# First attention phase: GpSimd subtracts the row maximum before the transposes, ScalarE applies the exponential behind them, and builds the masked queries

## The reference, cut to what matters

```python
scores = einsum('bhqd,bhkd->bhqk', qh, kh) + mask          # layer 0
scores = where(mask == 0, -inf, clip(scores * scale, -100, 100))   # layer 1
weights = softmax(scores, axis=-1)
ctx = einsum('bhqk,bhkd->bhqd', weights, vh)
```

## Time and profile before

| | us |
|---|---|
| runs of the kernel before | 2157.89, 2166.70, 2175.78 |
| their median | 2166.70 |
| span of the profiled execution, first to last instruction | 2161.6 |
| median less span | 5.1 |
| first phase in that execution | about 46 to 875 |

### The profile page before, as it was taken

How to read it: one execution, slowest core, us unless ns; L and a number is a source line. 1 busy time by engine, 2 the same in 40 slices (tenths; PEclk the granted TensorE clock), 3 DMA queues, 4 the chain that set the end, 5 groups by cost and what they waited for, 6 DMA issues and landing times.

```text
span 2161.6 us, 49950 instructions
## 1 busy us (share of the span) xinstructions
PE 1864.7 (86%) x17665; PEld 1517.8 (70%) x17669; DVE 1485.2 (69%) x3873; ACT 1300.1 (60%) x4466; POOL 616.4 (29%) x610
## 2 busy tenths in 40 slices
PE   3987988888889999648788989999999998898878
PEld 2776877777778777536666667777787777676765
DVE  5887776786877888566776676776767565564456
ACT  1886655565556688436677766666666654554432
POOL 0003021241312230014343434244353533333221
PEclk9998999999999999867799999999999999999999
DMA  8013334463444310210000011232222223232351
GB/s 240 17 31 102 106 114 144 130 180 96 141 128 140 102 31 7 96 64 20 24 25 2 20 39 33 83 92 66 89 62 80 82 70 105 61 96 79 99 155 51
DMA packets 119637, 178.44 MB, mean 83 GB/s; under 512 B 9824, under 2 KB 77728, under 8 KB 119136
## 3 DMA queue, kind: packets, MB, share of 16 engines
q1 hardware_dynamic: 111712, 159.51, 24.6%
q0 software_dynamic: 7680, 15.74, 2.5%
HBM read 141.26 MB, written 33.95 MB: 81 GB/s over the span
## 4 chain that ended last, share of the span: by engine, by line
PE 37%; DVE 9%; ACT 5%; issue 4%; POOL 1%; DMA 0%; DVEq 0%; ACTq 0%; SPq 0%
PE ps L1659 5%; PE ps L1944 5%; PE ps L1892 3%; PE ps L1697 3%; PE ps L1885 3%; ACT pb L2093 2%; PE ps L1681 2%; PE ps L1866 2%; PE ps L1688 2%; PE ps L1670 2%; PE ps L1707 1%; DVE nm L2472 1%; PE ps L1715 1%; PE ps L1914 1%; PE ps L1858 1%
## 5 line engine op out<-in xcount | busy, mean ns | idle before, releaser
L2093 ACT ACTIVATE pb<-ps,nm 128x128 f32<-128x128 f32 x1024 | 363.2, 377 | 194.1 <-DVE nm L2472 194.0
L2141 POOL TENSOR_TENSOR pb<-pb,rcs 128x512 f32<-128x512 f32 x256 | 267.8, 1047 | 661.6 <-DVE rcs L2480 660.8
L981 ACT ACTIVATE pb<-pb,nm 128x128 f32<-128x128 f32 x1024 | 313.0, 393 | 52.1 <-DVE nm L1206 50.6
L2497 DVE COPY pt<-ps 128x512 f32<-128x512 f32 x128 | 88.2, 689 | 198.0 <-PE ps L1944 197.9
L2093 ACT ACTIVATION_READ_ACCUMULATOR pb<-ps,nm 128x1 f32 x1024 | 221.8, 217 | 0.0
L2472 DVE TENSOR_REDUCE nm<-ps 128x8 f32<-128x1024 f32 x128 | 155.8, 1217 | 61.9 <-PE ps L1892 38.7
L1944 PE MATMUL ps<-w,pb 128*128 128x128 f32 x1024 | 168.3, 290 | 21.4 <-ACT pt L2101 10.2
L1206 DVE TENSOR_REDUCE nm<-pb 128x8 f32<-128x1024 f32 x128 | 156.1, 1220 | 4.4
L1944 PEld LDWEIGHTS ps<-w,pb 128*128 128x128 f32 x1024 | 122.2, 148 | 45.1 <-ACT pt L2101 19.3
L865 PE MATMUL ps<-w,pb 128*128 128x128 f32 x1024 | 146.0, 286 | 6.8 <-ACT pb L981 6.6
L2101 ACT ACTIVATE pt<-ps 128x512 f32<-128x512 f32 x128 | 76.9, 601 | 92.9 <-PE ps L1944 92.8
(11 more groups left out here) (379 smaller groups left out, 4415.6 us busy)
## 6 DMA issues: line engine op xcount, KB each, us to landing
big<-in_we SPq DMA_DIRECT2D x92, 514.0 KB, 3.7
big<-in_we SPq DMA_DIRECT2D x109, 384.0 KB, 3.1
sorted_out<-big SPq DMA_DIRECT2D x27, 256.0 KB
big<-sorted_in SPq DMA_DIRECT2D x7, 960.0 KB, 5.8
sorted_in<-big SPq DMA_DIRECT2D x4, 1472.0 KB, 12.2
hidden<-h_all SPq DMA_DIRECT2D x7, 512.0 KB, 3.0
h_all<-hidden SPq DMA_DIRECT2D x7, 512.0 KB, 3.8
sorted_out<-h_all SPq DMA_DIRECT2D x14, 256.0 KB
```

What stands on the lines that cost most here:

```text
L981: m = a.activation(pb[:, n % 2, k * S:(k + 1) * S], pb[:, n % 2, k * S:(k + 1) * S], ACT.Exp, bias=nm[:, n % 2, k:k + 1])
L2093: m = a.activation(pb[:, n % 2, e * S:(e + 1) * S], ps[:, score_bank(n) + half, k * S:(k + 1) * S], ACT.Exp, bias=nm[:, n % 2, e:e + 1], a ...
L2141: g_.tensor_tensor(p4, p4, r4.unsqueeze(2).to_broadcast([P, 4, S]), ALU.mult).then_inc(n2["p_normed"], 1)
L2497: v.tensor_copy(pt[:, p % 2, 4 * S:8 * S], ps[:, BANK_T, :]).then_inc(n2["p_lo"], 1)
```

## The change

- GpSimd adds nm to pb, in place, for each half of a unit (new function `shift`, semaphore `shifted`), at the head of its loop's turn n.
- PE's transposes wait for `shifted` in place of `exps`; so does DVE's maximum, which reuses nm.
- ACT's eight exponentials of a unit are gone. It empties both banks of the transposed values with Exp, in all units; DVE's copy is gone.
- `queries` moves from DVE to ACT, to place 2 of u = 4 (layer 0) or u = 6 (layer 1).
- The gathers, so far all at u = 0, stand at u = 0, 1 and 2 (2, 3 and 3 of them). The scatters, so far four in each of u = 4 to 7, are three in each of six units from unit 27 (then 43, 59, 75) on; the sixth has one.

```diff
+        GATHERS = {0: range(0, 2), 1: range(2, 5), 2: range(5, 8)}
+        SCATTERS = [range(3 * i, min(3 * i + 3, 2 * PB)) for i in range(6)]
+        SCATTERS_FROM = 3 * NU + 3
@@ PE @@
-                                pe.wait_ge(s["exps"], 2 * p + 1 + k // 4)
+                                pe.wait_ge(s["shifted"], 2 * p + 1 + k // 4)
@@ ACT @@
+                    if layer == 0 and here == (2, 4):
+                        queries(j + 1, (front.yT_ready, g + 1), W("hm"))
+                    if layer == 1 and here == (2, 6):
+                        queries(j + 1, (s["q_col"], g + 1), W("hms"))
+                def queries(j, there, heads_mask):
+                    a.wait_ge(*there)
+                    if j >= 2:
+                        a.wait_ge(s["scores"], NU * (j - 1))
+                    for i in range(4):
+                        m = a.activation(qms[j % 2][:, i, :], qT[:, :], ACT.Copy, scale=heads_mask[:, i:i + 1])
+                    m.then_inc(s["q_ready"], 1)
-                        a.activation(pt[:, p % 2, 0:4 * S], ps[:, 2, :], ACT.Copy).then_inc(s["p_hi"], 1)
-                        if not any(tiles_at(place, n) for place in range(3)):
-                            a.wait_ge(s["transposed"], 2 * p + 2)
-                            a.activation(pt[:, p % 2, 4 * S:8 * S], ps[:, 3, :], ACT.Copy).then_inc(s["p_lo"], 1)
+                        a.activation(pt[:, p % 2, 0:4 * S], ps[:, 2, :], ACT.Exp).then_inc(s["p_hi"], 1)
+                        a.wait_ge(s["transposed"], 2 * p + 2)
+                        a.activation(pt[:, p % 2, 4 * S:8 * S], ps[:, 3, :], ACT.Exp).then_inc(s["p_lo"], 1)
-                    if n < NUN:
-                        a.wait_ge(s["maxed"], n + 1)
-                        for k in range(BLK):
-                            m = a.activation(pb[:, n % 2, k * S:(k + 1) * S], pb[:, n % 2, k * S:(k + 1) * S], ACT.Exp,
-                                             bias=nm[:, n % 2, k:k + 1])
-                            if k % 4 == 3:
-                                m.then_inc(s["exps"], 1)
@@ POOL @@
+                def shift(n):
+                    g_.wait_ge(s["maxed"], n + 1)
+                    for half in range(2):
+                        p4 = pb[:, n % 2, 4 * half * S:4 * (half + 1) * S].rearrange("p (k s) -> p k s", k=4)
+                        m4 = nm[:, n % 2, 4 * half:4 * half + 4]
+                        g_.tensor_tensor(p4, p4, m4.unsqueeze(2).to_broadcast([P, 4, S]), ALU.add)\
+                            .then_inc(s["shifted"], 1)
                 for n in range(NUN + 2 * NU):
                     j, u = divmod(n, NU)
+                    if n < NUN:
+                        shift(n)
                     layer, g = stream(j + 1)
-                    if layer == 1 and u == 0:
+                    if layer == 1 and u in GATHERS:
...
-                        for k in range(2 * G):
+                        for k in GATHERS[u]:
...
-                    layer, g = stream(j - 2)
-                    if layer == 0 and g % 2 and u >= 4:
-                        p = g // 2
-                        if u == 4:
+                    p, at = divmod(n - SCATTERS_FROM, 2 * NU)
+                    if 0 <= p < NP and at < len(SCATTERS):
+                        if at == 0:
...
-                        for k in range(4 * (u - 4), 4 * (u - 3)):
+                        for k in SCATTERS[at]:
@@ DVE @@
-                        queries(j + 1, (front.yT_ready, g + 1), W("hm"))
-                        queries(j + 1, (s["q_col"], g + 1), W("hms"))
-                            v.wait_ge(s["exps"], 2 * (n - 1))
+                            v.wait_ge(s["shifted"], 2 * (n - 1))
-                    if 0 <= n - 1 < NUN and any(tiles_at(place, n) for place in range(3)):
-                        p = n - 1
-                        v.wait_ge(s["transposed"], 2 * p + 2)
-                        if p >= 2:
-                            v.wait_ge(s["pv"], p - 1)
-                        v.tensor_copy(pt[:, p % 2, 4 * S:8 * S], ps[:, 3, :]).then_inc(s["p_lo"], 1)
```

More of the change, by code:

```diff
@@ L298, in build @@
                       "p_lo", "pv", "o_recip", "normed", "oT_psum", "oT_ready", "out_psum", "bias_added"]
-        att_a = attention_sems("a", both_kinds + ["q_ready", "masked", "o_read", "o_turned"])
+        att_a = attention_sems("a", both_kinds + ["q_ready", "masked", "shifted", "o_read", "o_turned"])
         att_b = dict(att_a, **attention_sems("b", ["sums_turned", "p_normed", "k3_psum", "k3_col", "v_row", "chunk_added",
@@ L956, in work @@
                         tile(*item)
+                def queries(j, there, heads_mask):
[5 more added lines that the diff above has]
+                    m.then_inc(s["q_ready"], 1)
                 a.wait_ge(front.yT_psum, 1)
                 a.activation(qT[:, :], ps[:, 6, :], ACT.Copy).then_inc(front.yT_ready, 1)
+                queries(0, (front.yT_ready, 1), W("hm"))
                 for n in range(NUN + 2 * NU):
@@ L1002, in _ @@
                     j, u = divmod(n, NU)
+                    if n < NUN:
+                        shift(n)
                     layer, g = stream(j + 1)
-                    if layer == 1 and u == 0:
-                        g_.wait_ge(moe["stored"], 16 * NQ0 * (g // 2 + 1))
-                        if g:
-                            g_.wait_ge(moe["gathered"], 16 * 2 * G * g)
-                            g_.wait_ge(moe["combined"], g)
-                        for k in range(2 * G):
+                    if layer == 1 and u in GATHERS:
+                        if u == 0:
+                            g_.wait_ge(moe["stored"], 16 * NQ0 * (g // 2 + 1))
+                            if g:
+                                g_.wait_ge(moe["gathered"], 16 * 2 * G * g)
+                                g_.wait_ge(moe["combined"], g)
+                        for k in GATHERS[u]:
                             e = k // G * PB + g % 2 * G + k % G
@@ L1050, in apply @@
                     layernorm_apply_dve(v, f, n)
-                def queries(j, there, heads_mask):
-                    v.wait_ge(*there)
-                    if j >= 2:
-                        v.wait_ge(s["scores"], NU * (j - 1))
-                    for i in range(4):
-                        m = v.tensor_scalar(qms[j % 2][:, i, :], qT[:, :], heads_mask[:, i:i + 1], None, ALU.mult)
-                    m.then_inc(s["q_ready"], 1)
                 def tile(g, kind, t):
@@ L1095, in work @@
                         apply(front, g, g + 1)
-                    if layer == 0 and here == (3, 4):
-                        queries(j + 1, (front.yT_ready, g + 1), W("hm"))
                     if layer == 1 and here == (3, 1):
@@ L1115, in work @@
                         apply(late, g, g + 1)
-                    if layer == 1 and here == (3, 6):
-                        queries(j + 1, (s["q_col"], g + 1), W("hms"))
                     layer, g = stream(j - 1)
@@ L1174, in _ @@
                 apply(front, 0, 1)
-                queries(0, (front.yT_ready, 1), W("hm"))
                 for n in range(NUN + 2 * NU):
```

## The result

The changed kernel takes 2223.7 us (median of 4 runs, 2213.5 to 2230.9). Beside it on the same chip the kernel before took 2171.2 us: the ratio is 1.0257, 95% interval 1.0205 to 1.0309. It is slower by 2.6%, and the time lies above the predicted range (2146 to 2214). The profiled execution took 2213.5 us, with a span of 2211.7.

A forecast was written before the change was run, and what follows sets the result against it. TensorE was taken to bound the kernel, its 94.7 us idle in the first phase being about all to win. Losses of 42 less gains of 29 gave +13, 2175 on the span, 2180 us as median; range 2146 to 2214.

The forecast's parts named there:

- both halves block VectorE: Rival, first phase: both additions of a shift block VectorE, 2.1 us each meeting, 59 in place of 18; 2221 us, chance 0.20.
- VectorE beside GpSimd: First phase: VectorE operations on SBUF tensors lose 0.85 us beside a shift, in 17 units without tiles and 45 with: +18.
- The sign that I had named: Sign that the forecast is right: the stage from unit 34 to 101 keeps its length within 15 us.
- The power behind the shift: Seven first-layer units: GpSimd's layer norm power comes after the shift, so VectorE's apply waits and P times V starts late: +9.
- Gathers: Last two groups: gathers queue between shifts, so the combination starts late, 5.5 us taken twice: +11.
- Scatters: Units 27 to 32: DMAs queue with three shifts, so the sorted rows TensorE waits for come later: +3.6 us.
- Start: Very start of the phase: nothing hides the four masked query products, now on ScalarE: +0.6 us.
- The gains: First phase: exponentials' wait 6.6, ScalarE's late y 4, VectorE's copy 14 and masked products 4, together 29 us.
- a late y: ScalarE's step for a new y (L929) no longer queues behind eight exponentials: -4 of TensorE's 5.1 us wait.
- The shift itself: Every unit: two GpSimd additions of 1.04 us each; an undisturbed unit stays at 3.78 us and the wait for exponentials goes.

The follow-up runs named there:

- The idle additions: Kernel before, plus two GpSimd additions of constants behind each unit's maximum, into tiles nobody reads or waits for: 2215.5 us, ratio 1.0189.
- The copy alone: Kernel before with both halves of every evacuation on ScalarE, VectorE's copy in tile units gone, exponentials still on ScalarE: 2165.9 us, ratio 1.0002.
- the queries alone: Kernel before with only the masked queries moved from VectorE to ScalarE: 2190.2 us, ratio 1.0095.
- the fills: Changed kernel without the shift, GpSimd making four fills of 128x512 with zeros a unit in its place: 2194.5 us, ratio 1.0103.
- the run with idle additions: Changed kernel without the shift, GpSimd making two additions of constants a unit in its place, nobody waiting for them: 2215.0 us, ratio 1.0203.

## Why the prediction was wrong, by its steps

The mechanisms were all there; the forecast of 2180 failed on one share and one cover. The branch it called "both halves block VectorE" gave 2221, next to the measured 2223.7, though partly by luck: it charged 2.1 us for each meeting, 59 us in all, where a group of four applies lost 1.46 (2.57 for 1.12) and some 36 us come out below, and it charged too little for the power and the gathers.

- **"VectorE beside GpSimd", +18: the step that failed.** The raw amount was right: 62 meetings of 0.85 us are 52.7 us, and 46.0 were measured. Wrong was what it costs. "I let 0.6 of it reach TensorE in the first and a quarter in the second", a third over all (18 of 52.7). The idle additions turned 27 of 60.3 us of stretch into pauses of TensorE, 0.45, and another 20 us, 0.33, into slower work behind the pauses. Outside the tiles the end came 34 us later for some 36 of stretch, where I allowed 0.6, and among tiles 13 later for some 24, where I allowed a quarter. At four fifths, the share over the phase, the term is 36. The sign that I had named, a stage from unit 34 to 101 within 15 us of its length, held (541 for 533): the loss lies mostly in the stages without tiles. The step lacked the clock altogether: the prediction read TensorE's idle time as "about all that can be won", and its busy time as fixed.
- The rule of the Trainium skill (SBUF — State Buffer, "SBUF: two separate sides") that the later of the two engines blocks fully, for a whole instruction, gave +45 in the prediction, and the trace agrees for single instructions: each addition held one apply for about its whole length (1.07 and 1.08 us), but a group lost 1.46 us and not 2.1. I had set it aside because the median of a later row was undisturbed (278 ns). Of its 128 instructions 94 met no addition, and none of these took over 0.29 us; of the other 34, 16 took 0.70 to 1.13.
- **The power behind the shift, +9: mechanism right, cover too large.** VectorE waited up to 3.2 us, as predicted, in seven units (20.0 us in all), and P times V of unit 9 started at 91.91 us: the predicted 90.3 and the 1.6 by which that unit began later. But the maxima, 1.6 us behind the kernel before at unit 9, were 5.3 behind at unit 12, 3.7 where the step had 2.1; what came on top came while TensorE worked at a clock of 0.71 and 0.81. Taking the wait away brought 12 to 20 us (medians, ratios) although the applies then stretched by 9.8 us more (55.8 for 46.0).
- **Gathers, +11:** the combination waited 14.7 us in 5 groups; the last two groups lost 2.7 and 4.0 us (9.81 for 7.09, 11.12 for 7.10), less than the 5.5 each charged. **Scatters, +3.6:** not seen; TensorE's wait for sorted rows fell from 16.0 to 10.5. **Start, +0.6:** the first maximum is 0.1 us late.
- **The gains, -29:** 24 measured, as a whole. Their parts were not what I wrote. The copy alone gave 0 (charged 14), the queries alone cost 20 (charged a gain of 4). That fits a gain that comes from ScalarE's time, which the prediction valued at 4 us for a late y, and only once the exponentials are gone; it is argued, not shown, for how the 24 divide was not tried further.
- **The shift itself:** 1.05 us an addition and 3.75 us an undisturbed unit, as predicted, and waiting for it costs little.

The sum with measured terms: gains 24; blocking 36; power and gathers some 30 of their 34.7 us of waits (an estimate from the fills). That is +42 of the 47 by which the stages grew and the 52.5 between the medians. The rest I can't assign: waiting for the shift itself accounts for at most 12 of it by the run with idle additions, whose own last maximum is even later than the changed kernel's (924.1 for 911.5 us).

## What to carry to other kernels

Before moving an elementwise step to GpSimd, list what VectorE does in the same microseconds. Here each addition held an operation that reads and writes SBUF alone for most of the addition's length (0.73 us of 1.05 lost per addition by the applies), while those that read PSUM, reductions and statistics went on. A stretch on a chain that passes through VectorE each unit was not covered by VectorE's idle time: nearly all of it reached the end in the units that TensorE fills, and about half among the tiles. Where TensorE bounds the kernel a pause can cost twice, once idle and once at the lower clock that follows, so charge a delay at close to its full length even where half is covered. And try the parts of a change singly: here two reliefs were worth nothing or less alone, and the change without its additions 24 us.

## What the runs showed of the hardware

- Each of two GpSimd additions in a row held one VectorE apply: four applies took 2.57 us around 2.07 us of additions, and 1.12 us without. Four instructions of the changed kernel's phase were held through both additions (2.46 to 2.86 us). Even an operation on 128x4 elements (L336 of the front layer norm, 0.17 us) took 0.70 us on average.
- A fill, which reads nothing, holds VectorE up as well, but less: 19.2 us of stretch for 2.1 us of fills a unit against 44.5 for 2.1 us of additions. The combination, whose two large operands both lie in SBUF, kept its time: 17 of its 64 instructions ran beside a fill and took 352 ns at most, where 8 that met an addition in the changed kernel took 0.76 us on average.
- The reduction over 128x1024 in SBUF (1220 ns) and masking out of PSUM (1217 to 1219 ns) kept their mean within 10 ns beside additions in every run.
- A power on 128x4 elements takes GpSimd 1.02 us, as long as an addition of 128x512 (1.05), so it fills a queue as much.
- On VectorE the same addition took 0.69 us.
- TensorE's busy time for the same 7890 matmuls of the phase ran from 726 us (no shift, mean granted clock 0.96) over 734 (before, 0.96) and 759 (the change, 0.93) to 767 (idle additions in the shift's place, 0.90): what the other engines delay changes how fast TensorE works, not only when.
